# A graph layer and a top-2 expert layer on one core: input roots and products move between VectorE and GpSimd, loads between queues, and the last batch's tail is ordered anew

## The reference, cut to what matters

```python
h = layernorm(x)                                   # x: 8 batches, 1024 rows, 128 features
q, k, v = (h @ W.T + b for each of Wq, Wk, Wv)     # 4 heads of 32
scores = clip(q k^T / sqrt(32), -10, 10), in 8 chunks of 128 keys
scores = where(mask == 0, -10, scores)
attn = softmax(scores) inside each chunk           # 8 softmaxes a row
ctx = sum over the chunks of attn @ v
x1 = x + layernorm(ctx @ Wo.T + bo + h) * gamma + beta
y = layernorm(x1); probs = softmax(y @ gate_w + gate_b); best two of 8 experts
out = x1 + sum over the two of prob * (gelu(y @ W1 + b1) @ W2 + b2)
```

## Time and profile before

| | us |
|---|---|
| median of 3 runs (lowest to highest) | 817.09 (816.98 to 817.26) |
| profiled execution, its time | 815.88 |
| profiled execution, its span | 814.1 |
| busy: TensorE, VectorE, ScalarE, GpSimd | 665.5, 675.7, 559.2, 552.4 |

### The profile page before, as it was taken

How to read it: one execution, slowest core, us unless ns; L and a number is a source line. 1 busy time by engine, 2 the same in 40 slices (tenths; PEclk the granted TensorE clock), 3 DMA queues, 4 the chain that set the end, 5 groups by cost and what they waited for, 6 DMA issues and landing times.

```text
span 814.1 us, 20184 instructions
## 1 busy us (share of the span) xinstructions
PE 665.5 (82%) x6427; PEld 382.6 (47%) x6427; DVE 675.7 (83%) x1701; ACT 559.2 (69%) x1091; POOL 552.4 (68%) x567
## 2 busy tenths in 40 slices
PE   4598499999699999999999885685330699999994
PEld 1333134434234334334344232463220699999994
DVE  4989989989599899899899996786572498888893
ACT  4697397995797997988989865654300577777772
POOL 1210818787699899898998999867877155555554
PEclk9999899999899999999999998766555699999998
DMA  8826105446425326236154200401111222232210
GB/s 275 245 82 165 67 26 166 138 114 167 116 69 177 104 93 167 76 116 161 66 152 134 78 22 0 104 28 45 44 51 54 52 69 65 82 82 78 63 47 3
DMA packets 60700, 78.22 MB, mean 96 GB/s; under 512 B 8229, under 2 KB 33666, under 8 KB 60595
## 3 DMA queue, kind: packets, MB, share of 16 engines
q1 hardware_dynamic: 42962, 45.26, 18.4%
q10 hardware_dynamic: 12672, 23.07, 10.6%
q0 software_dynamic: 4960, 8.58, 3.3%
HBM read 56.05 MB, written 22.59 MB: 97 GB/s over the span
## 4 chain that ended last, share of the span: by engine, by line
PE 34%; ACT 18%; DVE 14%; POOL 13%; issue 8%; DMA 8%; ACTq 3%; SPq 1%; POOLq 0%; DVEq 0%
DMA qk_dram<-qk_lo 6%; POOL rows_dram L627 6%; ACT w L776 5%; PE score_ps L1558 4%; ACT prob_ring L776 4%; PE sum_ps L1572 4%; PE side_ps L1588 3%; ACT ctx_sb L756 3%; POOL ctx_sb L566 3%; PE score_ps L1516 3%; ACTq L742 3%; PE score_ps L1518 3%; PE score_ps L1517 3%; ACT xn L698 2%; PE sum_ps L1798 2%
## 5 line engine op out<-in xcount | busy, mean ns | idle before, releaser
L1007 DVE SCALAR_TENSOR_TENSOR prob_ring<-score_ps,limit 128x1024 f32<-128x1024 f32 x128 | 149.5, 1209 | 17.0 <-PE score_ps L1558 16.6
L776 ACT ACTIVATE prob_ring<-prob_ring 128x1024 f32<-128x1024 f32 x128 | 133.1, 1056 | 40.6 <-DVE prob_ring L1007 22.4
L1558 PE MATMUL score_ps<-stack_mem 128*128 128x512 f16 x512 | 140.3, 389 | 25.0 <-DVE prob_ring L1007 19.6
L1007 DVE SCALAR_TENSOR_TENSOR w<-score_ps,limit 128x1024 f32<-128x1024 f32 x128 | 149.9, 1214 | 8.7 <-PE score_ps L1558 8.4
L566 POOL TENSOR_TENSOR ctx_sb<-ctx_sb,rspread 128x512 f32<-128x512 f32 x108 | 139.2, 1289 | 23.6 <-POOL ctx_acc L571 9.5
L776 ACT ACTIVATE w<-w 128x1024 f32<-128x1024 f32 x128 | 134.1, 1055 | 28.7 <-issue 14.0
L634 POOL DMA_INDIRECT out_x<-xn,limit x91 | 90.3, 992 | 86.3 <-DVE xn L1395 71.1
L571 POOL TENSOR_TENSOR ctx_acc<-ctx_acc,ctx_sb 128x512 f32<-128x512 f32 x93 | 118.9, 1278 | 7.3
L901 ACT ACTIVATE xn<-score_ps,vec 128x128 f32<-128x128 f32 x364 | 99.4, 385 | 11.6 <-PE score_ps L1518 10.6
L1558 PEld LDWEIGHTS score_ps<-stack_mem 128*128 128x128 f16 x512 | 37.7, 98 | 125.1 <-issue 49.5
L627 POOL DMA_INDIRECT rows_dram<-x,limit x64 | 65.1, 1017 | 27.6 <-issue 19.0
(11 more groups left out here) (240 smaller groups left out, 1583.8 us busy)
## 6 DMA issues: line engine op xcount, KB each, us to landing
rspread<-rinv_dram SPq DMA_DIRECT2D x84, 256.0 KB
stack_mem<-qk_dram ACTq DMA_DIRECT2D x56, 256.0 KB, 4.7
ctx_sb<-rows_dram SPq DMA_DIRECT2D x91, 66.5 KB, 2.0
qk_dram<-qk_hi ACTq DMA_DIRECT2D x16, 256.0 KB, 2.8
qk_dram<-qk_lo ACTq DMA_DIRECT2D x16, 256.0 KB, 5.9
x<-in_adj SPq DMA_DIRECT2D x4, 512.0 KB, 7.6
ctx_sb<-in_adj SPq DMA_DIRECT2D x4, 512.0 KB, 10.0
stack_mem<-qk_dram SPq DMA_DIRECT2D x16, 128.0 KB, 3.2
```

The costliest lines, as they stand in the source:

```text
L776: act.activation(prob_at(s, u), prob_at(s, u), ACT.Exp, scale=1.0 / SCORE).then_inc(exp_done, 1)
L1007: dve.scalar_tensor_tensor(out=prob_at(s, u), in0=score_ps[:, 2 * u:2 * u + 2, :], scalar=-LIMIT * SCORE, in1=limit[:, k:k + 1, half * HAL ...
L1558: ins = pe.matmul(score_ps[:, h, :], kstack[:, par, h, k * P:k * P + P], qstack[:, par, h, half * HALF:half * HALF + HALF], start=True, st ...
```

## The change

- **Input norm.** Four groups of batches {0}, {1}, {2, 3}, {4 to 7}. All but the first have their variance made by VectorE's `bn_aggr` (8 for each batch, `prep_moments`) and their root by one power on GpSimd (`prep_root`). The stats of batches 2 and 3 move into batch 0 at s = 0, 1, those of 4 and 5 to s = 13, 15, those of 6 and 7 into batch 1. The bias parts and the constants' copies move from the start to batch 0, s = 9.
- **Start.** q is stored after its own two parts are made, k before the v copies; SyncE loads q's stacks behind q's store alone. Four of eight mask turns and copies move from the start into steps 0 and 1.
- **Stacks.** The loads that stack q and k move from ScalarE's queue to SyncE's, between the factors of group 2b-1 and 2b. `begin_rows` moves to before the loop.
- **Last batch.** Groups 14 and 15 hold its steps 0 to 7, four each; two of each four are loaded and two shuffled. GpSimd does steps 0 to 7 alone, VectorE the products of 8 to 15 and seven sums. The gate has six sets {0}, {1}, {2, 3}, {4, 5}, {6}, {7}, the first right behind the loop. ScalarE's scalings of these halves (`post_y`, `x2`) are ordered to match.

```diff
-    GATED = (range(0, 1), range(1, 3), range(3, 5), range(5, 7), range(7, 8))
+    GATED = (range(0, 1), range(1, 2), range(2, 4), range(4, 6), range(6, 7), range(7, 8))
...
-        BATCHES = (range(0, 1), range(1, NB - 4), range(NB - 4, NB))
+        BATCHES = (range(0, 1), range(1, 2), range(2, NB - 4), range(NB - 4, NB))
+        EARLY = 4
...
-            sp.wait_ge(parts_stored, 64)
             for c in range(2):
                 for i in (c, 1 - c):
+                    if c == 0:
+                        sp.wait_ge(parts_stored[i], 32)
...
+            load_x(3)
+            sp.wait_ge(consts_ready, CONSTS)
+            zeros_and_ones = gather[:, :, :].rearrange("p j d -> p (j d)")
+            for r in range(PAIRS + 1):
+                sp.dma_start(rows_dram[CAP * r:CAP * r + P, :], zeros_and_ones[:, 0:ROW]).then_inc(rows_begun, 16)
+            def stack_parts(bb, i):
+                sp.wait_ge(parts_stored[i], 32 * bb + 32)
+                wait(sp, qk_done, 2 * STEPS * (bb - 1))
+                dst, order = stacks_of(i)
+                for r, part in enumerate(order):
+                    sp.dma_start(dst[DH * r:DH * r + DH, bb % 2, :, :],
+                                 qk_dram[2 * i + part].rearrange("(h d) n -> d h n", h=HEADS)).then_inc(stacked, 16)
+            def load_spreads(G):
                 sp.wait_ge(rinv_ready, G + 1)
                 sp.dma_start(rinv_dram[G % 2], rinv[:]).then_inc(rinv_stored, 16)
                 sp.wait_ge(rinv_stored, 16 * (G + 1))
-                for j in range(SHUFFLED, GROUP):
-                    g = STARTS[G] + j
+                for g in range(STARTS[G], STARTS[G + 1]):
+                    if not loaded(g):
+                        continue
                     wait(sp, chunk_added, g - SPREADS + 1)
+                    j = g - STARTS[G]
                     sp.dma_start(rspread[:, g % SPREADS, :],
                                  rinv_dram[G % 2].rearrange("(h j c) n -> h j (c n)", h=HEADS, c=2)[:, j:j + 1, :]
                                  .to_broadcast([HEADS, DH, HALF])).then_inc(rspread_loaded[g % SPREADS], 16)
-                if G == 2:
-                    begin_rows()
+            for b in range(NB):
+                if b:
+                    load_spreads(2 * b - 1)
+                if b < LAST:
+                    stack_parts(b + 1, 0)
+                    stack_parts(b + 1, 1)
+                    load_spreads(2 * b)
+            for G in range(2 * LAST, STORED):
+                load_spreads(G)
...
+            def prep_root(i):
+                rows = x1_rows(BATCHES[i].start, BATCHES[i].stop)
+                rstd, shift = rows[:, :, RSTD], rows[:, :, SHIFT]
+                pool.wait_ge(moments_ready, i)
+                pool.tensor_scalar(rstd, rstd, EPS, 1.0, ALU.add, ALU.mult).then_inc(prep_root_step, 1)
+                pool.tensor_scalar(shift, shift, -1.0, 1.0, ALU.mult, ALU.mult)
+                pool.wait_ge(prep_root_step, 2 * i - 1)
+                pool.tensor_tensor(rstd, rstd, neg_half[:, 0:1].to_broadcast([P, T * len(BATCHES[i])]), ALU.pow).then_inc(prep_root_step, 1)
+                pool.wait_ge(prep_root_step, 2 * i)
+                pool.tensor_tensor(shift, shift, rstd, ALU.mult).then_inc(shift_ready, 1)
+            prep_root(1)
...
+                    if s == 5 and first:
+                        prep_root(2)
+                    if s == 15 and second:
+                        prep_root(3)
...
                 qk_high(0, i, i % 2)
+                if i == 2:
+                    store_parts(0, 0)
+            store_parts(0, 1)
             for c in range(2):
                 v_copy(0, 0, c, c)
-            for i in range(2):
-                store_parts(0, i)
-            for k in range(T):
+            def limit_copy(k):
                 act.wait_ge(mask_turned, k + 1)
                 act.activation(limit[:, k, :], side(k % 2).bitcast(BF16), ACT.Copy,
                                bias=-LIMIT * SCORE).then_inc(limit_ready, 1)
+            for k in range(EARLY):
+                limit_copy(k)
...
             post_root(2 * LAST - 1)
-            normalise(LAST, STEPS - 8)
-            normalise(LAST, STEPS - 7)
-            normalise(LAST, STEPS - 6)
-            normalise(LAST, STEPS - 5)
+            root3(5)
             post_final(LAST - 1, 1)
+            scatter(range(0, T))
+            root3(6)
+            scatter(range(T, 2 * T))
             post_root(2 * LAST)
-            scatter(range(0, T))
-            root3(5)
-            root3(6)
-            scatter(range(T, 3 * T))
+            scatter(range(2 * T, 4 * T))
             post_root(2 * LAST + 1)
-            scatter(range(3 * T, 4 * T))
+            scatter(range(4 * T, 5 * T))
             root3(7)
-            scatter(range(4 * T, TILES))
+            scatter(range(5 * T, TILES))
...
-                        if s in (8, 10):
-                            stack_parts(b + 1, 1 - par, (s - 8) // 2)
-                        if s in (6, 8):
-                            store_parts(b + 1, (s - 6) // 2)
-                    if s == 0 and not last:
-                        prep_xn(b + 1, range(0 if first else TH, T))
+                        if s - first in (6, 8):
+                            store_parts(b + 1, (s - first - 6) // 2)
+                    if s == 0 and not first and not last:
+                        prep_xn(b + 1, range(TH, T))
+                    if s in (1, 2) and first:
+                        prep_xn(b + 1, range((s - 1) * TH, s * TH))
                     if s == STEPS - 1 and b + 2 < NB:
                         prep_xn(b + 2, range(TH))
                     if s == 3 and not first and not second:
-                    if s in (12, 13) and not first:
+                    if s in (12, 13) and not first and not last:
-                    if s in (14, 15) and last:
+                    if s in (10, 11) and last:
...
+            def prep_moments(i, batches):
+                for bb in batches:
+                    dve.wait_ge(norm_step, STAT_STEPS + bb)
+                    for t in range(T):
+                        ins = dve.bn_aggr(x1_rows(bb)[:, t, SHIFT:SHIFT + 2], stats[:, (bb - batches_at(i)) * T + t, :])
                 if batches[-1] == BATCHES[i][-1]:
-                    ins.then_inc(norm_step, 1)
-            def prep_rsqrt(i):
-                span = slice(BATCHES[i].start * T, BATCHES[i].stop * T)
+                    ins.then_inc(moments_ready, 1)
...
-                    if first and s in (9, 10, 11, 13):
-                        i = (9, 10, 11, 13).index(s)
-                        prep_stats(2, BATCHES[2][i:i + 1])
-                    if first and s == 14:
-                        prep_rsqrt(2)
+                    if first and s in (0, 1):
+                        prep_stats(2, BATCHES[2][s:s + 1])
+                    if first and s in (2, 3):
+                        prep_moments(2, BATCHES[2][s - 2:s - 1])
+                    if first and s == 9:
+                        bias_parts()
+                        copy_consts()
+                    if first and s in (13, 15):
+                        prep_stats(3, BATCHES[3][s // 15:s // 15 + 1])
+                    if second and s in (0, 8):
+                        prep_stats(3, BATCHES[3][2 + s // 8:3 + s // 8])
+                    if second and s in (1, 7, 10, 13):
+                        prep_moments(3, BATCHES[3][(1, 7, 10, 13).index(s):(1, 7, 10, 13).index(s) + 1])
...
+            def late_products(steps):
+                for s in steps:
+                    dve.wait_ge(ctx_copied, STEPS * LAST + s + 1)
+                    dve.tensor_tensor(late_context(s), late_context(s), rspread[:, s % SPREADS, :], ALU.mult).then_inc(tail_step, 1)
+            def late_sums():
+                total = late_context(T)
+                for k in range(1, T):
+                    dve.wait_ge(tail_step, T + k - 1)
+                    last = k == T - 1
+                    if last:
+                        dve.wait_ge(chunk_added, STEPS * LAST + T)
+                        dve.wait_ge(wo_done, 2 * LAST)
+                    ins = dve.tensor_tensor(ctxT[:, 1, :] if last else total, total, late_context(T + k), ALU.add)
+                    ins.then_inc(chunk_added if last else tail_step, T if last else 1)
...
+            stats_of(5)
+            gate_logits(0)
             invert(len(SIZES) - 1)
-            for j in range(TAIL):
-                spread(LAST, STEPS - TAIL + j)
+            gate_choice(0)
+            late_products(range(T, T + TAIL))
+            gate_slots(0)
+            gate_logits(1)
+            gate_choice(1)
+            stats_of(6)
+            gate_slots(1)
+            gate_logits(2)
             post_res(LAST, 0)
             post_stats(2 * LAST)
             post_moments(2 * LAST)
-            gate_logits(0)
-            stats_of(5)
-            gate_choice(0)
-            last_products()
-            gate_slots(0)
-            last_sums()
```

(31 more changed lines are left out.)

182 lines of the change are left out of this document (80 added, 102 removed).

## The result

| | before | after |
|---|---|---|
| median, us (lowest to highest) | 817.17 (816.98 to 818.19) | 792.02 (789.99 to 792.67) |
| profiled execution, span | 814.1 | 790.2 |

What follows compares the result with a forecast made beforehand. VectorE was taken to set the pace, busy 52.0 of 55.2 us in batch 4, TensorE following closely. Terms -3.2 - 9.3 + 3.2 - 8.7 - 4 - 8 = -30.0 gave 785.9 us profiled, 787 median; range 776 to 800.

Steps and rivals of the forecast that it cites:

- Batch 2, the zeros: Batch 2: VectorE's 8.67 us wait for scores, traced to late zeros and a blocked ScalarE queue, goes; -8.7 us.
- Either alone would do: Batch 2: moving the zeros, or taking the stack loads' wait off ScalarE's queue, would each remove the 8.67 us wait.
- Batch 0: Batch 0: the 11.7 us Newton chain on VectorE goes, 2.4 us of aggregates and small operations come in; -9.3 us.
- Batch 1: Batch 1: 5.4 us of statistics and aggregates added on VectorE, less a 2.2 us wait that goes; +3.2 us.
- Start: Before the first scores: four q stack loads issue earlier and the last store stands ahead of v copies; -3.2 us.
- Batches 3 to 6: Batches 3 to 6: 1 us back in each of the 3.2 us that VectorE does not work; -4 us.
- Tail: Batch 7 and behind the loop: first scatter at 521 instead of 534.30, then 99.3 us of scatters; -8 us.
- (a): Rival: tail gives nothing back because VectorE is the bound through all six sets; 795 us, chance 0.18.
- (b): Rival: no contention at set 0, smaller waits between sets, batches 3 to 6 give 7; 780 us, chance 0.12.
- (c): Rival: stack loads on SyncE's queue become the bound, k issued late at seven handovers; over 818 us, chance 0.04.
- the sign "over 2 us": Prediction is wrong if a batch's first scores wait on stack_mem by over 2 us, the mark of (c).
- (d): Rival: zeros ahead of the loop delay batch 0's first factors, so the 8.67 us moves; 796 us, chance 0.03.

Runs made afterwards that it cites:

- e1: Kernel before, with only the 29 stores of zeros moved ahead of the loop on SyncE's queue; 807.1 us against 815.5, ratio 0.9886.
- i2: Changed kernel with statistics of batches 4 to 7 in batch 0 and their GpSimd root early in batch 1; 818.5 us on a slower chip, ratio 0.9753 to before.
- e2: Changed kernel with the 29 stores of zeros put back behind group 2's factors; 826.6 us on a slower chip, ratio 0.9848 to the kernel before.
- e3: Kernel before, with the chain for batches 4 to 7 replaced by 32 VectorE aggregates and one GpSimd power in batch 1; 802.6 us, ratio 0.983.
- e5: Changed kernel with the last batch's part put back as before (five gated sets, old products and tail order); 794.2 us, ratio 0.9734 to the kernel before.
- r1: Changed kernel again, unedited, in another measurement; 790.8 us, ratio 0.968 to the kernel before.
- c1: Changed kernel with the edits of i2 and i3 together; 780.9 us, ratio 0.9551 to the kernel before.
- c2: As c1, but VectorE waits for GpSimd's last root before clearing ctxT and splitting the first expert weights; 779.3 us, ratio 0.9543 to the kernel before.
- i3: Changed kernel with VectorE's calls behind the loop reordered (late products, residuals and moments, last final); 814.8 us on a slower chip, ratio 0.9712 to the kernel before.

## Why the prediction was right, and where its sizes were off

The two largest terms, batch 0's chain and batch 2's zeros, had the right cause and nearly the right size; each was tested alone. Of what is missing in the sum, the tail is the largest piece in the first profile (3.9 us), its size nearly twice too large. Misses also cancelled, which is luck: batch 1 cost 2.8 us less than forecast, and that covers what batches 0 and 2 fell short (1.7 and 1.3).

- **Batch 2, the zeros: right in cause and nearly in size** (e1: -9.4, forecast -8.7). But the change gives 2.9 to 4.5 of it back in the same batch (56.8 and 58.4 against i2's 53.9), which the prediction did not see: it placed "GpSimd's roots for these batches" in "its slack" by the busy time of batch 1. The root at step 15 fell on the beginning of batch 2, where GpSimd, busy 53.0 of 56.8, is the bound (i2). The step priced the root at nothing and named no duration for 32 columns; it takes 5.5.
- **"Either alone would do": wrong** (e2). Moving the stack loads alone moves the stall to batch 3. The forecast was saved by the change doing both, and that was luck.
- **Batch 0: right.** By itself the chain, less the aggregates in its place, is worth 9.6 (e3), 9.5 by the sum. In the whole change the batch fell by 7.6 to 9.4, the more the higher TensorE's clock in the first steps was (e5, where the clock was full, has 9.4 against the 9.3 of the forecast). The sum has no term for that clock.
- **Batch 1: the term was mis-sized**, +3.2 for +0.4. VectorE's busy time rose by 4.7 (50.35 to 55.03; 5.4 forecast), but of the 4.9 us that it had idle in this batch 4.3 went, where the sum took 2.2.
- **Start: -1.3 or -3.3, forecast -3.2.** The size goes with how long the q store takes to land, since the stack loads wait for it. In this profile it took 7.50 us, in r1 5.28 for the same code; in the kernel before the last store took 3.55, and the sum has no term for a longer landing. The store now runs while the adjacency is still being loaded; that this is what makes it slow was not tested.
- **Batches 3 to 6: -3.3 and -5.0, forecast -4.** Right in size, open in cause: no run moves the stack loads alone, and e3, which leaves them on ScalarE's queue, has some -1.7 in these batches.
- **Who sets the pace.** The prediction gives it to VectorE (52.0 of 55.2 in batch 4), though its own row has TensorE busy 53.5. The shortest batches of these runs took 53.9, with TensorE busy 53.35 and VectorE 51.60 (i2, batch 2). So TensorE is at least as near to being the bound of such a batch; no run separates the two.
- **Tail: the step that failed in size.** The first scatter was right to half a microsecond (79.3 against 78.9 from the batch's first clip). The stretch of scatters was forecast at 99.3 and took 104.2. The waits between them came to 8.5 (3.51, 4.68, 0.33), 9.4 forecast. What was missing: the last root took 5.6 and not 2.5, kept standing by VectorE's large operations, as c1 and c2 show for another operation of the same root; and the first six scatters of set 2 (the third, batches 2 and 3) have a pitch of 1.4 to 1.7 beside VectorE's products and sums, not 1.277, which is 1.4 in all. That second part was not tested by itself, and some 1.3 us are spread over small pieces.
- **Rivals.** (a) was forecast for a VectorE that is the bound through all sets. i3 shows the half of it: VectorE's order, not its amount, made GpSimd wait. (b), smaller waits between the sets and no contention, did not come. (c) did not come: in the changed kernel TensorE waited for stacks once, 3.6 us, and that was for the very first scores, not at a handover between batches. By its letter the sign "over 2 us" was met there. (d) did not come: in r1 the zeros were issued by 56.0, and the first factors only at 76.6.
- **The other signs.** GpSimd's last sum of step 7's half ended at 492.2, 19 us earlier on the clock and not 22, but 69.3 from the batch's first clip, as before: no gap of its own. GpSimd waited 5.8 us for slots in all, under the 12 named. Batch 2 (56.8) lay outside its 54 to 55.

## What to carry to other kernels

Price a moved operation on the engine it goes to, at the place where it lands, with its own size: the engine's share of the batch before says nothing about the next. When work moves out of one stage, add up all the stages that it touched: batches 1 and 2 alone show 5.7 us for i2's edit in c1, and batch 0 was 5.1 longer there. Fill an engine's wait for another with calls that a third one waits for, as in i3, before counting how much work each has. When a burst of transfers (here 29) goes out on a queue, look for its damage up to 20 us later and on other queues, and move the burst.

## What was not expected of the hardware

- A small GpSimd operation (128x8, 0.21 us) took 2.75 us (c1) and another of its kind 3.40 (the changed kernel) while VectorE ran 128x1024 operations with both operands in SBUF. It took 0.21 once VectorE was made to wait (c2). The Trainium skill, "SBUF — State Buffer", section "SBUF: two separate sides", calls the pair of ports that VectorE and GpSimd share an exclusive lock; the runs agree, and show GpSimd as the one that waits, which the prediction counted for VectorE alone.
- The same code in the same steps had TensorE granted 0.70, 0.80 or 1.00 of its clock on average between 33 and 50 us, in different runs, and batch 0 took 57.7, 56.7 and 55.9 (the changed kernel twice, and e5).
- The power on GpSimd took 1.7 us for 8 columns, 2.9 for 16 and 5.5 for 32 (i2), so nearly by columns: 0.16 us for each, and some 0.4 besides.
- On one of the chips the expert stage took 201.5 us and not 181, the way from the last scatter to the first load 10 and not 2.4, and the attention's batches what they take elsewhere.
